# A graph layer with eight experts on one core: two places for the experts' output, used by even and odd experts, and a GpSimd wait one expert further back

## The reference, cut to what matters

```python
xn = layernorm(x)                                      # x is 1250 x 768
x = x + gnn(xn, edges) + attention(xn)                 # called x1 below
xf = layernorm(x)
probs = softmax(xf @ switch_w + switch_b)              # 8 experts
prob_max, routes = max(probs), argmax(probs)
# up to 195 rows of an expert, those of the highest prob_max, are kept
h = gelu(einsum('ecd,edf->ecf', buf, w1) + b1)         # 768 -> 384
o = einsum('ecf,efd->ecd', h, w2) + b2                 # 384 -> 768
y = where(keep, o[routes, rank], xf)
return x + y * prob_max
```

## Time and profile before

| what | us |
|---|---|
| median of 3 runs | 1019.64 (1017.2 to 1021.0) |
| the profiled execution, its own time | 1020.73 |
| its span in the trace | 1019.0 |
| PE busy | 906.3 (89% of the span) |
| DVE busy | 760.4 (75%) |
| ACT busy | 488.4 (48%) |
| POOL busy | 359.7 (35%) |

### The profile page before, as it was taken

How to read it: one execution, slowest core, us unless ns; L and a number is a source line. 1 busy time by engine, 2 the same in 40 slices (tenths; PEclk the granted TensorE clock), 3 DMA queues, 4 the chain that set the end, 5 groups by cost and what they waited for, 6 DMA issues and landing times.

```text
span 1019.0 us, 15414 instructions
## 1 busy us (share of the span) xinstructions
PE 906.3 (89%) x5154; PEld 859.9 (84%) x5154; DVE 760.4 (75%) x1570; ACT 488.4 (48%) x720; POOL 359.7 (35%) x236
## 2 busy tenths in 40 slices
PE   2899789989989989999999899979999995499895
PEld 2899689989989989988988789969999995398884
DVE  6778459989989989989988798554666666567773
ACT  2221256766766766767667641340323222255540
POOL 1014455545445554654555620000000001526562
PEclk9899799999999999999999899998999995599998
DMA  9986462364464364355436379255676634767861
GB/s 275 353 146 176 93 123 32 65 114 81 63 114 81 60 113 78 59 110 83 66 44 146 57 118 207 60 147 129 186 204 183 168 122 132 213 200 239 273 203 47
DMA packets 137614, 136.70 MB, mean 134 GB/s; under 512 B 70561, under 2 KB 118276, under 8 KB 136545
## 3 DMA queue, kind: packets, MB, share of 16 engines
q1 hardware_dynamic: 109646, 119.29, 44.9%
q0 software_dynamic: 27520, 16.67, 11.7%
q10 hardware_dynamic: 403, 0.17, 0.1%
HBM read 94.31 MB, written 38.17 MB: 130 GB/s over the span
## 4 chain that ended last, share of the span: by engine, by line
PE 55%; DVE 18%; issue 11%; DMA 7%; ACT 5%; POOL 1%; SPq 1%; DVEq 0%; ACTq 0%; POOLq 0%
PE ps L2027 9%; PE ps L2028 9%; PE ps L2029 9%; PE ps L1202 7%; PE ps L1186 4%; PE ps L1187 4%; PE ps L1623 3%; DMA out<-oE,ids 3%; DVE Pl L1061 3%; PE ps L1624 3%; DVE Ph L1059 2%; ACT Ph L852 2%; DMA Cs<-counts 2%; PE ps L1162 1%; ACT Pf L874 1%
## 5 line engine op out<-in xcount | busy, mean ns | idle before, releaser
L388 POOL DMA_INDIRECT counts<-countc,idxu x157 | 274.3, 1747 | 258.6 <-DMA counts<-countc,idxu 222.5
L1061 DVE SCALAR_TENSOR_TENSOR Pl<-Pf,Ph 125x832 fp32r<-125x832 f32 (+1 forms) x180 | 184.2, 1027 | 44.0 <-ACT Ph L852 40.4
L874 ACT ACTIVATE Pf<-ps 125x832 f32<-125x832 f32 (+1 forms) x180 | 156.0, 867 | 127.2 <-PE ps L1187 119.1
L1202 PE MATMUL ps<-Ph,vsb 125*128 125x416 f32 (+1 forms) x360 | 133.4, 371 | 23.2 <-DVE Pl L1061 23.0
L1202 PE MATMUL ps<-Pl,vsb 125*128 125x416 f32 (+1 forms) x360 | 127.9, 355 | 0.0
L1202 PEld LDWEIGHTS ps<-Ph,vsb 125*128 125x128 f32 x360 | 68.6, 191 | 39.1 <-DVE Pl L1061 26.0
L2027 PE MATMUL ps<-wH,XH 128*125 128x384 f32 x240 | 84.5, 352 | 4.1 <-DVE wL L481 4.1
L2027 PE MATMUL ps<-XH,wqkH 128*128 128x416 f32 (+1 forms) x216 | 83.1, 385 | 4.4 <-DVE wqkL L299 2.4
L2028 PE MATMUL ps<-wL,XH 128*125 128x384 f32 x240 | 82.9, 346 | 0.0
L2029 PE MATMUL ps<-wH,XL 128*125 128x384 f32 x240 | 82.6, 344 | 0.0
L852 ACT ACTIVATE Ph<-Pf 125x832 fp32r<-125x832 f32 (+1 forms) x90 | 80.5, 895 | 0.8
(11 more groups left out here) (281 smaller groups left out, 2196.2 us busy)
## 6 DMA issues: line engine op xcount, KB each, us to landing
Cs<-counts SPq DMA_DIRECT2D x17, 546.9 KB
w1s<-L_ffn_w SPq DMA_DIRECT2D x8, 1152.0 KB, 6.4
w2s<-L_ffn_w SPq DMA_DIRECT2D x8, 1152.0 KB
odram<-OHL SPq DMA_DIRECT2D x12, 625.0 KB, 8.4
oS<-odram SPq DMA_DIRECT2D x10, 750.0 KB, 4.8
vdram<-VS SPq DMA_DIRECT2D x10, 672.0 KB
vsb<-vdram SPq DMA_DIRECT2D x12, 560.0 KB
kt<-keyd SPq DMA_DIRECT2D x5, 1280.0 KB
```

Of the source, the lines that this page charges most:

```text
L388: pool.indirect_dma_start(out=counts, out_offset=bass.IndirectOffsetOnAxis(ap=idxu[:, c:c + 1], axis=0), in_=countc[:, c:c + 1], in_offset ...
L874: act.activation(Pf[:, i % RING, :, 0:w], ps[0:T, 2 * (i % 2):2 * (i % 2) + 2, 0:w], ACT.Square, bias=1.0).then_inc(sq_done, 1)
L1061: dve.scalar_tensor_tensor(out=p, in0=f, scalar=1.0, in1=h.bitcast(F32), op0=ALU.add, op1=ALU.subtract).then_inc(p_lo, 1)
L1202: ins = pe.matmul(ps[:, 4 + s % 2, 0:w], vsb[:, 2 * kp + t, a, :], part[:, m % RING, t, 0:w], start=(kp == 0 and t == 0 and part is Ph), s ...
```

## The change

A second place for the output is the first part of `XF`: `answer(0)` is `oE`, and `answer(1)` is `XF[0:105, 0:2, :]`. Even experts use the first, odd ones the second, in both DVE steps and in the scatter. GpSimd raises `oe_store` by 2 at its start instead of 1. At the end of expert e (1 to 6) it waits until the scatters of expert e-1 have landed, instead of those of e, and raises `oe_store`; after expert 0 it no longer waits. DVE has one more wait ahead of the experts, for the stores of `XF`.

```diff
+        def answer(b):
+
+            return (oE, XF)[b][0:CROWS, 0:2, :]
...
             pool.wait_ge(pads, 1)
-            pool.sem_inc(oe_store, FREE)
+            pool.sem_inc(oe_store, FREE + 1)
...
-                                            in_=oE[0:n, t, :], in_offset=None, bounds_check=N - 1, oob_is_err=False
+                                            in_=answer(e % 2)[0:n, t, :], in_offset=None, bounds_check=N - 1, oob_is_err=False
                                             ).then_inc(sent_out, 16)
...
-                if e + 1 < E:
-                    pool.wait_ge(sent_out, 32 * e + 32)
+                if 1 <= e < E - 1:
+                    pool.wait_ge(sent_out, 32 * e)
                     pool.sem_inc(oe_store, 1)
...
+            dve.wait_ge(xf_store, MOVED * NT)
             dve.sem_inc(y_done, FREE)
...
-                        dve.tensor_tensor(oE[0:n, t, :].rearrange("p (c d) -> p c d", c=2),
+                        y = answer(b)[0:n, t, :]
+                        dve.tensor_tensor(y.rearrange("p (c d) -> p c d", c=2),
...
-                        dve.scalar_tensor_tensor(out=oE[0:n, t, :], in0=oE[0:n, t, :], scalar=pcur[0:n, b, t:t + 1],
+                        dve.scalar_tensor_tensor(out=y, in0=y, scalar=pcur[0:n, b, t:t + 1],
```

## The result

| | before | after |
|---|---|---|
| median of 20 runs, us | 1019.38 (1011.16 to 1025.31) | 1008.32 (1000.22 to 1017.73) |
| ratio | | 0.9893, 95% interval 0.9864 to 0.9921 |
| the profiled execution, its own time | 1020.73 | 1012.63 |
| its span | 1019.0 | 1010.9 |
| turns of experts 1 to 5, together | 77.68 | 70.93 |

The mean of the four is 0.9905, that is 9.7 us.

A forecast was written before the change was run, and what follows sets the result against it. GpSimd's loop of scatter landing and issues was taken to bound the experts' turns at 15.48 us. Removing 5.3 of PE idle, 1.7 of lower clock, 0.3 of late gather and 0.4 of restarts, 7.7 us, gave 1011.9 us (range 1009.5 to 1016.5).

The forecast's parts named there:

- What bounds the kernel: Experts' stage: GpSimd's loop of scatter landing, semaphore and issues sets the turn at 15.48 us; DVE's bias and PE wait.
- The turn without the loop, 14.0: Turns of experts 1 to 5: five of 14.0 us, 70.0 where 77.68 stood, so 7.7 us less.
- The sign "13.9 to 14.1 us apart": Sign of being right: PE's transposes 13.9 to 14.1 us apart in the turns of experts 1 to 5.
- The clock as a term of 1.7 us: PE's lower clock from 922 to 926 us, 1.7 us, counted as gone with the 1.72 us idle ahead of it.
- The rival that priced the clock at 1.7 us: The steps hold, but PE's clock still falls once, 1.7 us of half clock: 1013.6 us, chance 0.08.
- GpSimd's spare time: GpSimd's queue: `xe` gathers leave 3.4 us after the transposes, early; semaphore has 3.6 us to spare; cost 0.
- Gathers of `x1g`: Ahead of DVE's second step: first in time even at worst, second at worst 2.7 us late; bound 0 to 0.3 us.
- DVE's added wait and the other place: DVE's wait for the stores of `XF`, and `XF` in place of `oE`: cost 0 each.
- GpSimd holds DVE: Running `xe` gathers delay `w2L` by 0.85 us in each of five turns, 4.3 us: 1016.2 us, chance 0.06.
- DMA becomes the bound: Load of `w1s` lands in 9.7 us beside the `xe` gathers, turns 14.7 us: 1015.4 us, chance 0.12.
- Slower: At L1857, `w1s` lands after 11.0 us, turns 16.0 us, clock falls in three turns: 1025.3 us, chance 0.05.
- The range, and the sum under it: Whole kernel: 1019.64 - 7.7 = 1011.9 us; range 1009.5 to 1016.5, below which a turn must be under 13.6.

The follow-up runs named there:

- the four: The changed kernel compared with the kernel before four times: ratios 0.9893, 0.9894, 0.9926 and 0.9905.
- before_2: The unchanged kernel before, profiled a third time: stage 77.38 us, ratio 0.9985.
- after_2: The changed kernel run a third time, nothing else altered: stage 69.86 us, ratio 0.9926 to the kernel before.
- after_extra_pool: The changed kernel with one GpSimd memset more (1.38 us and 0.3 of issue) in experts 1 to 6: stage 76.12 us, ratio 0.9976 to the kernel before.
- two_places_early_2: The changed kernel with the gathers of `xe` one expert further ahead, run a second time: stage 69.96 us, ratio 0.9913 to the kernel before.
- two_places_old_waits: The kernel before with the two output places only, GpSimd's semaphore and wait left as before: stage 78.44 us, ratio 1.0018.
- two_places_sleep: The changed kernel, but GpSimd still waits at each expert's end for that expert's own scatters: stage 86.24 us, ratio 1.0099 to the kernel before.
- before_1: The unchanged kernel before, profiled a second time: stage 77.86 us, ratio 1.0012.

## Why the prediction was wrong, point by point

**What bounds the kernel**: right. GpSimd's loop set 15.5 us a turn. The second place alone takes nothing away (78.4 us, and 86.2 where the bias no longer waits but GpSimd still sleeps), GpSimd's wait off the queue alone takes 3.4 us (74.2), and both together 7.5 (70.2).

**The turn without the loop, 14.0**: right, and a little high. It is 13.93, set by PE and its short wait for `hL`; the stage of 77.68 went to 70.93, 69.65 and 69.86, so the term of 7.7 measured 6.75 in the first profile and 7.5 in the mean. The sign "13.9 to 14.1 us apart" did not hold of three turns in the first profile: 14.96, 13.54 and 14.57.

**The clock as a term of 1.7 us**: wrong as a part, harmless in the sum. before_2 has the loop and a full clock, and is 0.3 us shorter, not 1.7. Five turns of 15.5 less five of 14.0 is the whole of it; the half clock lay inside the loop's waits. In before_2 PE waits for the bias in all five turns, 6.5 us, where it waited 5.3 in four with the half clock. So 7.7 had the right size by the difference of the turns, and not by the parts it was split into. The rival that priced the clock at 1.7 us rested on the same step.

**GpSimd's spare time**: its queue did what was said, gathers at 3.4 us behind the transposes and the second held by `w2L`. But "early, for rows needed a turn later" was wrong in size: PE asks for those rows 10.7 us after the first issue (at 921.46). The second gather, held until 915.04, came 0.87 us late (922.33), and in after_2 0.48 us late once. I compared the semaphore with its deadline, and not the rows with theirs. after_extra_pool shows what that margin is.

**Gathers of `x1g`**: 0.25 us once, inside the bound of 0 to 0.3. That the first of them is in time even at its worst did not hold in a near relative: in two_places_early_2 it came 0.57 us late, held the bias of tile 1 and with it PE, and the turn was 0.35 us longer. **DVE's added wait and the other place**: no gain or cost that shows, 1.0018 (0.9984 to 1.0053) in two_places_old_waits.

**GpSimd holds DVE**: it does not. `w2L` started at 911.60 with a gather under way since 910.73, and took 2.56; the next gather took 2.96. The Trainium skill (SBUF — State Buffer, Who interferes with whom) lets the one that starts first block the other; for these instructions the traces show only GpSimd held.

**DMA becomes the bound**: partly seen. In one turn of the first profile, the one of 15.23 us in the table, ACT waited 6.18 us for `w1s`, which landed 11.2 us after its issue, `w1L` was 1.8 us late, and PE waited 1.0 instead of 0.35 us for `hL`. That is 0.65 us once, where 0.7 in each of five turns was priced.

```profile
932.40 2.13 ACT L1861 ACTIVATE w1H<-w1s 128x2304 fp32r<-128x2304 f32 x1 [6.18 <-DMA w1s<-L_ffn_w]
```

```profile
934.56 2.56 DVE L1907 TENSOR_TENSOR w1L<-w1s,w1H 128x2304 fp32r<-128x2304 f32 x1 [1.80 <-ACT w1H L1861]
```

**Slower**: the place was wrong. Not `w1s` but the rows of `xe` made turns of over 20 us, in two_places_sleep and the two kernels with the memset.

**The range, and the sum under it**: this is the step that failed. The sum took 7.7 us off the median of before and put everything outside the five turns at nothing, and the lower end of the range, 1009.5, rested on the same step ("below it a turn would have to be under 13.6"). No turn of the table is under 13.9, and the time was still 1008.3. Of the 11.1 us measured in the first comparison, the stage holds 6.75 in its profile and 7.5 in the mean of three. The noise was taken from three runs of before (1017.2 to 1021.0). Single runs of the two kernels spread over 14.2 and 17.5 us in the first comparison, whose ratio has an interval of 2.9 us to each side, and the four comparisons give 7.5 to 10.9 us by their ratios. So a part of the miss is a lower end drawn too close for this noise, and some 2.2 us over the 7.5 of the stage are left in the mean. The three comparisons of the kernels with the early gathers leave less, 9.4, 8.9 and 8.6 us where their stages are 8.0, 7.7 and 8.0 shorter. Whether the remainder is real, and where it would lie, stays open: the traces put nothing there that the change could have moved.

## What to carry to other kernels

Where a queue's owner sleeps for a landing, the turn can be the sum of that loop. Here neither a second buffer nor a moved wait alone took all of it away: free the buffer and the queue together. Give each gather behind it a deadline of its own, the time at which its rows are asked for, since a small delay of the queue can otherwise come back several times over; issuing it a turn earlier cost nothing here. A half clock or an idle that lies inside a loop's wait is no term of the sum, so price the loop once.

## What the runs showed of the hardware

Indirect DMAs of GpSimd, which are issued in 1.0 us, took up to 4.3 us, mostly 2.9 to 4.3, beside a `TENSOR_TENSOR` of DVE with both inputs in SBUF (`w1L`, `w2L`), and DVE's 2.55 us never grew (2.54 to 2.58 in all traces). A `SCALAR_TENSOR_TENSOR` with two inputs in SBUF did not hold them: in the changed kernel the scatter of 917.07 ran beside the one of 917.29 and took 1.00 us.

The clock did not fall behind each idle. It was at 0.50 after PE's 6.4 us in two_places_sleep. In the kernel before it fell after 1.72 us in one turn, while idles of 0.97 to 1.34 us in the same trace left it at 1.00. The length of the idle did not decide it alone: in before_1 it fell after 1.61 and after 1.45 us, and in before_2 an idle of 1.59 us left it at 1.00. At the lower level (1.2 GHz) the twelve transposes took 2.21 us, against 1.20.
